# Banded attention on one core: the band moves from matrix products to a VectorE add-and-maximum and a GpSimd affine select

## The reference, cut to what matters

```
x = transpose(mask)                      # positions x channels
q, k, v = split(x @ w_in.T + b_in)
scores = q @ k.T / sqrt(d)
band = abs(i - j) <= 64                  # local_size
scores = where(band, scores, most negative float)
attn = softmax(scores)
o = transpose(attn @ v @ w_out.T + b_out)
y = relu(o) * encodings
out = w_ct.T @ y + b_ct                  # then x = layernorm(x + out)
```

## Time and profile before

| | us |
|---|---|
| median of three runs | 3577.44 |
| profiled execution, its own time | 3583.71 |
| its span | 3581.8 |
| the stage: first S product to last result | 405.0 to 725.3 |
| S and C together | 441.1 to 690.3 |
| C alone | 690.3 to 713.6 |
| busy over the whole span: PE, VectorE, ScalarE, GpSimd | 3307.3, 2355.5, 1953.8, 1961.4 |

### The profile page before, as it was taken

How to read it: one execution, slowest core, us unless ns; L and a number is a source line. 1 busy time by engine, 2 the same in 40 slices (tenths; PEclk the granted TensorE clock), 3 DMA queues, 4 the chain that set the end, 5 groups by cost and what they waited for, 6 DMA issues and landing times. The chain is left out here.

```text
span 3581.8 us, 97201 instructions
## 1 busy us (share of the span) xinstructions
PE 3307.3 (92%) x37572; PEld 2307.7 (64%) x37572; DVE 2355.5 (66%) x4366; ACT 1953.8 (55%) x5232; POOL 1961.4 (55%) x2830
## 2 busy tenths in 40 slices
PE   8999699989699999999999999999998688679996
PEld 6777466656377777777777777777776355446665
DVE  5555266534488787788778878788877488534443
ACT  1111155522376776667776677667666277535555
POOL 3333333134466666666666666666666257657774
PEclk9999699989799999999999999999999699889998
DMA  2000444100211111111211111111110356366655
GB/s 83 12 12 9 111 116 115 37 26 1 64 51 42 57 51 51 51 42 49 58 54 42 51 48 54 51 51 51 48 39 29 84 150 171 110 206 211 214 182 227
DMA packets 223118, 278.45 MB, mean 78 GB/s; under 512 B 58548, under 2 KB 186872, under 8 KB 216280
## 3 DMA queue, kind: packets, MB, share of 16 engines
q1 hardware_dynamic: 203340, 237.24, 23.4%
q0 software_dynamic: 18432, 34.96, 2.8%
q10 hardware_dynamic: 908, 0.27, 0.1%
HBM read 162.13 MB, written 125.83 MB: 80 GB/s over the span
## 5 line engine op out<-in xcount | busy, mean ns | idle before, releaser
L2164 PE MATMUL head_ring<-gd_xT,head_w 128*128 128x512 f32 x1024 | 509.0, 620 | 11.8 <-DMA head_w<-gd_w 10.4
L1504 POOL DMA_INDIRECT ytok<-exp_arena,exp_cur x256 | 251.1, 981 | 119.3 <-issue 72.1
L2164 PEld LDWEIGHTS head_ring<-gd_xT,head_w 128*128 128x128 f32 x1024 | 175.7, 191 | 151.7 <-issue 135.8
L2467 DVE TENSOR_TENSOR head_Xs<-head_bx,head_join 128x512 bf16<-128x512 f32 x320 | 219.7, 686 | 81.3 <-PE head_bx L2205 81.3
L2436 DVE SCALAR_TENSOR_TENSOR head_cb_V<-head_ring,head_taps,head_cb_V 128x504 f32<-128x504 f32 (+2 forms) x384 | 263.0, 726 | 2.8 <-ACT head_cb_V L2312 2.8
L2284 PE MATMUL head_by<-head_wo,head_ogT 128*128 128x256 f32 x1016 | 255.0, 394 | 6.7 <-DVE rows_xc L2499 0.2
L2173 PE MATMUL head_ring<-head_w,gd_xT 128*128 128x256 f32 x1024 | 258.4, 396 | 0.0
L2284 PEld LDWEIGHTS head_by<-head_wo,head_ogT 128*128 128x128 f32 x1016 | 183.6, 190 | 37.0 <-DVE rows_xc L2499 13.7
L2173 PEld LDWEIGHTS head_ring<-head_w,gd_xT 128*128 128x128 f32 x1024 | 186.1, 192 | 32.5 <-issue 0.5
L2349 ACT CAST head_Tt<-head_btt 128x512 bf16<-128x512 f32 x320 | 194.1, 607 | 16.9 <-PE head_btt L2213 15.7
L1076 DVE TENSOR_REDUCE cf_top<-cf_near 128x4 f32<-128x1024 f32 x128 | 155.2, 1218 | 64.4 <-PE cf_near L917 62.7
(11 more groups left out here) (367 smaller groups left out, 9299.0 us busy)
## 6 DMA issues: line engine op xcount, KB each, us to landing
xbuf<-head_blank SPq DMA_DIRECT2D x64, 552.0 KB
exp_arena<-xbuf SPq DMA_DIRECT2D x64, 552.0 KB, 5.3
head_gi<-scan SPq DMA_DIRECT2D x64, 256.0 KB
ytok<-head_blank SPq DMA_DIRECT2D x64, 256.0 KB
exp_arena<-ytok SPq DMA_DIRECT2D x14, 1024.0 KB, 12.3
moe_w<-moe_w SPq DMA_DIRECT2D x32, 384.0 KB, 3.3
cb_Q<-qd SPq DMA_DIRECT2D x45, 192.0 KB
cb_K<-kd SPq DMA_DIRECT2D x45, 192.0 KB
```

Of the source, the lines that this page charges most:

```text
L1504: pool.indirect_dma_start(ytok, bass.IndirectOffsetOnAxis(ap=cur[i % AHEAD][s][:, b:b + 1], axis=0), y[i % RESULTS][s][:, b, :], None, bou ...
L2164: last = pe.matmul(b[:, :], w[:, c, FEAT[what]], xT[:, c, n % UNITS * N:n % UNITS * N + N], start=c == 0, stop=c == DC - 1)
L2467: dve.tensor_tensor((Ti if a == 0 else Xs)[:, :, :], bx[:, :].rearrange("p (q i) -> p q i", i=SEQ), join[:, a, :].unsqueeze(1).broadcast_t ...
```

## The change

The product with the band is taken out of S and out of C. In S, VectorE now runs per head and query tile one tensor_tensor_reduce: it adds the f32 band to 192 scores in PSUM, writes the sum back to the same place, and gives the maximum. In C the exponential is taken over all 384 columns, and GpSimd then sets those beyond the band to zero, four heads at a time, with four affine selects (new step M, one slot behind the last C of a group). V waits for M and stands 6 slots behind C. The band is no longer cast to bf16. Since the reduction can't negate, the three rows beside K hold -1.

near is now four buffers of one bank, prob one tile with a ring of 12, LAG 32; split is cut into five steps at -35, -33, -31, -29, -27, and the steps after V are 8 to 9 slots later.

```diff
-    SLOTS, RING, GROUP, LAG, FIRSTS = 4, 8, 4, 28, 4
+    SLOTS, RING, GROUP, LAG, FIRSTS, BEHIND = 4, 12, 4, 32, 4, 6
-    plan = {"prepare": -36, "split": -35, "spread": -28, ...
-            "place": 22, "unload": 45, "sort": 47, ... "close": 58, "store": 61}
+    plan = {"prepare": -36, "split0": -35, "split1": -33, ... "split4": -27, "spread": -28, ...
+            "place": 22, "unload": 53, "sort": 55, ... "close": 67, "store": 70}
-            if 0 <= g - LAG - 2 < UNITS and (g - LAG - 2) % GROUP == GROUP - 1:
-                yield "V", (g - LAG - 2) // GROUP
+            if 0 <= g - LAG - 1 < UNITS and (g - LAG - 1) % GROUP == GROUP - 1:
+                yield "M", (g - LAG - 1) // GROUP
+            if 0 <= g - LAG - BEHIND < UNITS and (g - LAG - BEHIND) % GROUP == GROUP - 1:
+                yield "V", (g - LAG - BEHIND) // GROUP
...
# PE, step S (C alike)
-                        pe.wait_ge(top_ready, since(n // 2 - 1))
-                        b = near[n // 2 % 2][:, n % 2 * 512:n % 2 * 512 + 512]
-                        pe.matmul(b[:, 0:QB * KW], ident16[:, :], band16[:, :], start=True, stop=False, ...)
+                        pe.wait_ge(top_ready, since(n - len(near) + 1))
+                        b = near[n % len(near)]
# PE, step V
-                        pe.wait_ge(prob_ready, since(n * GROUP + GROUP))
+                        pe.wait_ge(banded, since(n + 1))
# VectorE, step S
-                        dve.tensor_reduce(top[t % 2][:, :, j:j + 2]..., near[n // 2 % 2]..., AX.X, ALU.max, negate=True).then_inc(top_ready, 1)
+                        for i in range(QB):
+                            held = slice(i * KW, i * KW + KW)
+                            last = dve.tensor_tensor_reduce(out=near[n % len(near)][:, held], in0=near[n % len(near)][:, held], in1=band[:, held],
+                                                            scale=1.0, scalar=-3e38, op0=ALU.add, op1=ALU.max, accum_out=top[t % 2][:, i, j:j + 1])
+                        last.then_inc(top_ready, 1)
# GpSimd
+                    if what == "M":
+                        pool.wait_ge(prob_ready, since(n * GROUP + GROUP))
+                        held = slice(n * GROUP % RING, n * GROUP % RING + GROUP)
+                        for i, columns, up, base in ((0, slice(0, SEQ), 1, SEQ), (0, slice(SEQ, KW), -1, 0), (1, slice(0, P), 1, 0), (1, slice(P, KW), -1, 0)):
+                            kept = prob[:, held, i, columns]
+                            last = pool.affine_select(kept, kept, [[0, GROUP], [up, columns.stop - columns.start]], ALU.is_ge, nought,
+                                                      base=base, channel_multiplier=-up)
+                        last.then_inc(banded, 1)
```

More of the change, by code:

```diff
@@ L385, in stage_banded @@
     NEAR, FULL = PARTS * PARTS * DH, PARTS * PARTS * DH + PARTS
-    SLOTS, RING, GROUP, LAG, FIRSTS = 4, 8, 4, 28, 4
+    SLOTS, RING, GROUP, LAG, FIRSTS, BEHIND = 4, 12, 4, 32, 4, 6
     UNITS = TILES * H
     SCALE = float(np.float32(1.0) / np.sqrt(np.float32(DH)))
-    plan = {"prepare": -36, "split": -35, "spread": -28, "gather": -17, "values": -2, "fetch": -8, "tops": 17, "turn": 21,
-            "place": 22, "unload": 45, "sort": 47, "invert": 48, "ratio": 50, "wo": 54, "ct": 57, "close": 58, "store": 61}
+    plan = {"prepare": -36, "split0": -35, "split1": -33, "split2": -31, "split3": -29, "split4": -27, "spread": -28, "gather": -17, "values": -2, "fetch": -8, "tops": 17, "turn": 21,
+            "place": 22, "unload": 53, "sort": 55, "invert": 56, "ratio": 58, "wo": 63, "ct": 66, "close": 67, "store": 70}
     def timeline():
@@ L419, in stage_banded @@
         bv = m.sb("bv", [P, P])
-        band, band16 = m.sb("band", [P, QB * KW]), m.sb("band16", [P, QB * KW], BF16)
+        band = m.sb("band", [P, QB * KW])
         for name, t in (*w.items(), *bias.items()):
@@ L435, in stage_banded @@
         topT = [m.sb(f"topT{u}", [PARTS * H, T], BF16) for u in range(2)]
-        prob = [m.sb(f"prob{k_}", [P, KB, KW]) for k_ in range(RING)]
+        prob = m.sb("prob", [P, RING, KB, KW])
         oraw = [m.sb(f"oraw{u}", [P, 2, T]) for u in range(2)]
@@ L441, in stage_banded @@
         var, rstd = [m.sb(f"var{u}", [P, 1]) for u in range(2)], [m.sb(f"rstd{u}", [P, 1]) for u in range(2)]
-        near = [m.ps(f"near{k_}", (P, 1024)) for k_ in range(2)]
+        near = [m.ps(f"near{k_}") for k_ in range(4)]
         score = [m.ps(f"score{k_}") for k_ in range(2)]
@@ L654, in _ @@
                     u = n % 2
-                    if what == "S" and n % 2:
-                        t, j = n // H, n % H - 1
+                    if what == "S":
+                        t, j = n // H, n % H
                         dve.wait_ge(near_filled, since(n + 1))
                         dve.wait_ge(topsplit_step, since((t - 1) * SPLITS))
-                        dve.tensor_reduce(top[t % 2][:, :, j:j + 2].rearrange("p i j -> p j i"),
-                                          near[n // 2 % 2][:, :].rearrange("p (a k) -> p a k", a=2)[:, :, 0:QB * KW]
-                                          .rearrange("p a (i k) -> p a i k", i=QB),
-                                          AX.X, ALU.max, negate=True).then_inc(top_ready, 1)
+                        for i in range(QB):
+                            held = slice(i * KW, i * KW + KW)
+                            last = dve.tensor_tensor_reduce(out=near[n % len(near)][:, held], in0=near[n % len(near)][:, held], in1=band[:, held], scale=1.0, scalar=-3e38,
+                                                            op0=ALU.add, op1=ALU.max, accum_out=top[t % 2][:, i, j:j + 1])
+                        last.then_inc(top_ready, 1)
                     elif what == "values":
@@ L702, in prefill @@
                         last.then_inc(v_ones, 1)
+                nought = pool.to_reg(0.0)
                 for what, n in timeline():
                     u = n % 2
-                    if what == "split":
-                        pool.wait_ge(qk_ready, since(n + 1))
-                        if n >= 2:
-                            pool.wait_ge(spread_in[u], START + (n - 2) // 2 * WRITES + WRITES)
-                        left = qk[u]
-                        for i in range(PARTS):
-                            pool.wait_ge(split_step, since(n * SPLITS + 2 * i))
-                            pool.tensor_copy(part[u][:, i, :, :], left[:, :, :]).then_inc(split_step, 1)
-                            if i + 1 < PARTS:
-                                pool.wait_ge(split_step, since(n * SPLITS + 2 * i + 1))
-                                pool.tensor_tensor(rest[u][:, :, :], left[:, :, :], part[u][:, i, :, :], ALU.subtract).then_inc(split_step, 1)
-                                left = rest[u]
-                        if n == 0:
+                    if what == "M":
[6 more added lines that the diff above has]
+                        last.then_inc(banded, 1)
+                    elif what.startswith("split"):
+                        step, i = int(what[5:]), int(what[5:]) // 2
+                        pool.wait_ge(split_step, since(n * SPLITS + step))
+                        left = rest[u] if i else qk[u]
+                        if step == 0:
+                            pool.wait_ge(qk_ready, since(n + 1))
+                            if n >= 2:
+                                pool.wait_ge(spread_in[u], START + (n - 2) // 2 * WRITES + WRITES)
+                        if step % 2 == 0:
+                            pool.tensor_copy(part[u][:, i, :, :], left[:, :, :]).then_inc(split_step, 1)
+                        else:
+                            pool.tensor_tensor(rest[u][:, :, :], left[:, :, :], part[u][:, i, :, :], ALU.subtract).then_inc(split_step, 1)
+                        if (n, step) == (0, SPLITS - 1):
```

21 lines of the change are left out of this document (9 added, 12 removed).

## The result

| | before | after |
|---|---|---|
| median of 15 runs each, side by side, us | 3582.45 | 3570.6 |
| range of the runs | 3577.17 to 3589.98 | 3564.43 to 3579.11 |
| profiled execution, its own time (span) | 3583.71 (3581.8) | 3571.62 (3569.9) |

The ratio is 0.9965, 95% interval [0.9956, 0.9974]: by it 12.5 us faster (11.9 by the medians) where 23.4 were forecast. The direction came out and the time lies in the range; the size was taken nearly twice too large.

A forecast was written before the change was run, and what follows sets the result against it. PE was taken as the bound before, VectorE after. S with C 225.4 for 249.2, C alone 21.2 for 23.3, tail +2.5: -23.4 us, from 3583.7 to 3560.3 profiled, 3554 in the runs; range 3530 to 3618.

The forecast's parts named there:

- What the products cost PE: Two band products per unit, in S and C, leave PE: 0.17 us each, 5.3 of 17.5 us per tile.
- VectorE's pair: In S, add-and-maximum over 192 columns plus writing the maximum: 0.36 us taken, range 0.33 to 0.56, 32 per tile.
- The sentence that the prediction takes from the Trainium skill: Next VectorE instruction starts only once the pipe empties, putting the pair near 0.56 us; kept only as part of a rival.
- GpSimd's selects: In C, four affine selects per group of four heads: 2.0 us per group, GpSimd's tile then 15.3 us.
- Rival 1: GpSimd becomes the bound through step M's selects, from 2.55 us per group; slower, 3606 or 3654 us; chance 0.23.
- PE's clock stays: there it is 0.98 at that load.: PE's clock would hold during S with C, judged by the second channel attention, where no engine exceeds 85%.
- The sign that the prediction held for unlikely: PE at its lower clock of 1.2 GHz between 441 us and the end of S, listed as showing the forecast wrong.
- S with C: Stretch where S and C run together: 224 units at 1.006 us, 225.4 us for 249.2 before.
- I add 0.6 us: Per tile in S with C, for GpSimd's late root and four near banks: total 16.1 us per tile.
- The ends: Start and end of the stage: LAG 32 free at the start, C alone 21.2 us, tail +2.5 us.
- C alone: The 32 units of C left after S ends, 0.66 us each: 21.2 us for 23.3 before.
- The last stretch: After the last exponential, V now waits for the select, 2.0 us and a little: +2.5 us.

The follow-up runs named there:

- e5: Changed kernel with both band products and the two-head reductions kept as before, only plan, ring, LAG 32 and later steps new; 3576.14 us, ratio 0.9984.
- e3: Changed kernel with the band product and two-head reduction left in S, affine selects kept in C; 3552.41 us, ratio 0.9922.
- e1: Changed kernel without the four affine selects, so output is not the reference's; 3567.76 us, ratio 0.9966.
- e10: Changed kernel without affine selects, with redundant products added on PE; output is not the reference's; 3551.79 us, ratio 0.9913.
- e13: Changed kernel with redundant products on PE and every consumer of GpSimd's results placed later; 3695.3 us on another chip, ratio 0.9943.
- e7: Changed kernel with filler: two redundant 384-column products on PE in four slots of each tile; 3559.07 us, ratio 0.9935.

## Why the prediction was right in direction and wrong in size

- **What the products cost PE.** About right: e5 and e3, both at full clock, differ by one band product in each of 224 units and by 243.23 - 209.63 = 33.6 us of busy PE, 0.15 us each for 0.17 forecast.
- **VectorE's pair.** Its price was too high, 0.36 for 0.315 us. That hid the rest, and is luck: by 0.045 x 32 = 1.4 us per tile, some 20 us in 14 tiles, the stage should have been faster than forecast. (By the prediction's own sum the kernel is slower from a pair of 0.41 us on, not 0.40.) The write into PSUM cost nothing that shows. A pass starts together with the read of the one before, 0.08 us ahead of that pass's recorded end, as in the earlier trace rows. The sentence that the prediction takes from the Trainium skill (VectorE: DVE Perf Modes, The DRAIN you can't avoid) is only half of what stands there: the same paragraph goes on that a next instruction that isn't held starts earlier. With that the trace agrees.
- **GpSimd's selects.** The price was right (2.0 us per group). Rival 1 fell: GpSimd is busy 79%. Of the estimates from the Trainium skill (GPSIMD Engine Reference, Performance pitfalls for Q7 kernels), 2.6 us for a plain and 1.3 us for an unrolled loop, the measured 2.0 is neither.
- **"PE's clock stays: there it is 0.98 at that load." This step failed.** The second channel attention with its 85% was no guide to 83% here: 0.94, and 0.80 with 90% busy in e1 (busy time grows as the clock falls, so a busy share of a slowed PE says nothing on this). The sign that the prediction held for unlikely, 1.2 GHz in this stretch, came. The stage that it leaned on had a fall inside the very window of the earlier trace rows, with no wait of PE above 1.7 us near it; a mean of 0.98 hid it:

```profile
2900.00:2910.00 10.00, 8.13 (x70) 4.61 (x69) 8.25 (x16) 6.04 (x13) 7.14 (x9) 0.83 0.52 142
```

S with C came out at 233.7 us for 225.4. Filler gives back 5.3 of these 8.3 us, so the clock was more than half of the miss there; the other 3.0 (228.4 for 225.4) are what is left of the next step's error after the too high price of the pair.

- **"I add 0.6 us" for waits. This step failed too**, in size. VectorE was to be over 90% busy, 15.5 of 16.1 us per tile; it is busy 198 of 233.7. In the middle of the stage, at full clock (104 units are 6.5 tiles; first the changed kernel, then e10, 110 units), a tile takes 16.9 us and VectorE is busy for 14.8 of them, so waits are 2.1 us:

```profile
470.00:580.00 110.00, 87.67 (x977) 59.06 (x976) 96.23 (x485) 59.76 (x138) 92.97 (x192) 1.00 0.55 129
470.00:580.00 110.00, 100.84 (x1092) 67.49 (x1084) 100.00 (x511) 63.16 (x144) 44.95 (x91) 1.00 0.55 132
```

With the selects taken out and the filler in, a tile takes 16.0 us with VectorE busy for 14.5: 1.5 of waits. GpSimd's part of S with C is 11.7 us in these profiles, half of it lateness of its results (e13), for the other half no run separates a cause. That the remaining waits come from PE and VectorE passing only four near banks between them is argued, not shown.

- **The ends.** C alone missed by 1.6 us: without selects (e1, clock 1.00) it is the forecast's 21.2, with them at full clock (e3) 22.4, and 22.8 here at 0.93. The last stretch missed by 2.3. The last V begins 3.1 us behind the last exponential for 0.05 before, but 1.9 of that it has in e5 too, without any select, behind products of the tile before; the selects themselves add 1.3, not 2.0 and a little:

```profile
710.75 0.86 PE L592 MATMUL cb_out<-cb_prob,cb_V 128*32 128x192 f32 x16
```

(e5's last exponential ends at 708.88.) The remaining 1.7 of the 4.8 us are mostly PE's clock: its last products L600 and L608 take 1.97 and 1.19 us for 1.08 and 0.67 at the same place before. LAG was valued as four units moved; in e5 it earned more through an earlier start of the clock, in the changed kernel the clock came up later than before.

What stays open: which wait makes the clock fall, why half of the selects' cost remains when nobody is seen waiting for them, and where the gain of the filler beyond the stage comes from.

## What to carry to other kernels

Work taken off a PE that was full is worth less than its time once PE starts to wait: look at the granted clock per 10 us window, and take a clock below 1 as a cost of its own. A mean clock of another stage is no proof that yours will hold: look for falls inside it. Before one moves all such work, try half of it: here the band product of S left on PE beat the full change by 0.4%. A wait that is moved away from an engine that works in order mostly comes back at its next door, so test the wait's removal at an unchanged clock before believing in its gain.

## What the hardware showed that was not expected

- 128 redundant products more and a faster kernel: e7 against after, 0.9935 against 0.9965 (in the stage itself 3 to 5 us are shown); without selects, 16 us by the same filler.
- The granted clock fell to 1.2 GHz for some 7 us (0.66 in a 10 us window) in a stretch (S with C) in which PE never waited longer than 1.8 us.
- VectorE's pass isn't slowed by GpSimd's selects: median 394 ns with them (e7), 398 ns without (e10).
